# Sixteen-head attentions of a fused decoder: queries and keys projected without padded rows, each bank evicted twice

## Time and profile before

| | us |
|---|---|
| median of 3 runs | 2649.92 |
| lowest, highest | 2646.74, 2656.01 |
| profiled execution, own time | 2645.75 |
| its span (first to last instruction) | 2643.8 |
| PE busy in the span | 2145.4 (81%) |
| DVE busy | 1463.9 (55%) |
| ACT busy | 933.9 (35%) |
| POOL busy | 766.7 (29%) |

### The profile page before, as it was taken

The page is one execution under the profiler, slowest core; times in us unless marked ns, Lnnn a source line. Parts: engine busy times, 40 slices in busy tenths (PEclk is TensorE's granted clock), DMA queues, the critical chain, the costliest instruction groups (busy, mean ns, idle before and its releaser), DMA issues. The chain is left out here.

```text
span 2643.8 us, 37351 instructions
## 1 busy us (share of the span) xinstructions
PE 2145.4 (81%) x14118; PEld 1491.5 (56%) x14143; DVE 1463.9 (55%) x2966; ACT 933.9 (35%) x1539; POOL 766.7 (29%) x549
## 2 busy tenths in 40 slices
PE   7978857896498686499668877797999999687898
PEld 5765544564497575499345663485343434235787
DVE  4784773446432567311562454133799999993533
ACT  3423322331011234133323321111676667452543
POOL 1121231213200210100321011203489798973000
PEclk9999978998699687699789988898999999998899
DMA  4217010000697110698200002275201111001000
GB/s 161 73 41 248 17 34 32 1 2 33 236 358 297 58 33 8 233 358 320 66 1 25 1 2 89 80 213 154 88 25 40 31 34 40 25 1 52 1 17 16
DMA packets 104577, 234.22 MB, mean 89 GB/s; under 512 B 10000, under 2 KB 77456, under 8 KB 95440
## 3 DMA queue, kind: packets, MB, share of 16 engines
q1 hardware_dynamic: 95664, 209.81, 22.8%
q0 software_dynamic: 7680, 20.98, 2.4%
q10 hardware_dynamic: 1056, 1.05, 0.1%
HBM read 175.83 MB, written 55.97 MB: 88 GB/s over the span
## 5 line engine op out<-in xcount | busy, mean ns | idle before, releaser
L3631 POOL TENSOR_TENSOR l_attn_ring<-l_attn_ring,l_attn_c_rows 128x1024 f32<-128x1024 f32 x128 | 302.0, 2359 | 85.6 <-DVE l_attn_ring L3520 85.6
L3520 DVE TENSOR_TENSOR_SCAN l_attn_ring<-bank,l_attn_ring 128x512 f32<-128x512 f32 x256 | 299.2, 1210 | 22.6 <-ACT bank L3403 18.1
L164 PE MATMUL bank<-x_features,weights 128*128 128x512 f32 x544 | 260.5, 624 | 27.5 <-ACT x_features L3367 11.2
L3247 PE MATMUL bank<-l_attn_ring,identity 128*128 128x512 f32 x512 | 252.8, 617 | 36.8 <-POOL l_attn_ring L3631 29.8
L3403 ACT ACTIVATE bank<-l_attn_step,l_attn_minus_exp_a_log 128x508 f32<-128x508 f32 x256 | 173.5, 685 | 162.0 <-DVE l_attn_ring L3520 161.6
L164 PEld LDWEIGHTS bank<-x_features,weights 128*128 128x128 f32 x544 | 106.0, 199 | 155.5 <-issue 129.7
L3247 PEld LDWEIGHTS bank<-l_attn_ring,identity 128*128 128x128 f32 x512 | 96.6, 196 | 152.7 <-issue 105.2
L458 DVE TENSOR_REDUCE negmax_slots<-bank 128x16 f32<-128x2048 f32 x48 | 109.8, 2287 | 104.5 <-PE bank L350 104.2
L3514 DVE TENSOR_TENSOR l_attn_ring<-l_attn_step_times_input,bank 128x1024 f32<-128x1024 f32 x128 | 153.4, 1199 | 3.6 <-PE bank L3233 1.8
L3899 PE MATMUL bank<-l_ffn_hidden_high,l_ffn_sign_weights 128*128 128x512 f32 x256 | 99.7, 390 | 0.5 <-ACT l_ffn_hidden_high L3960 0.5
L3899 PE MATMUL bank<-l_ffn_hidden_low,l_ffn_sign_weights 128*128 128x512 f32 x256 | 99.6, 389 | 0.0
(11 more groups left out here) (678 smaller groups left out, 4486.4 us busy)
## 6 DMA issues: line engine op xcount, KB each, us to landing
l_attn_tile_weights<-l_ffn_experts SPq DMA_DIRECT2D x22, 2180.0 KB, 10.1
ffn_experts_tile_weights<-l_ffn_experts_experts SPq DMA_DIRECT2D x37, 1024.0 KB, 8.2
expert_slots<-zeros SPq DMA_DIRECT2D x8, 2048.0 KB, 13.6
l_attn_c_rows<-state_outputs SPq DMA_DIRECT2D x64, 256.0 KB, 3.2
l_ffn_tile_weights<-l_ffn_experts SPq DMA_DIRECT2D x23, 512.0 KB, 4.3
expert_slots<-residual_sum SPq DMA_DIRECT2D x62, 128.0 KB, 8.5
expert_slots<-zeros SPq DMA_DIRECT2D x1, 5888.0 KB, 27.8
l_ffn_tile_x<-expert_slots SPq DMA_DIRECT2D x23, 256.0 KB, 4.1
```

Source lines behind the costliest of these rows:

```text
L164: mm = pe.matmul(out, w[:, f, m * P:(m + 1) * P], src[:, f, :], start=start and f == 0, stop=stop and f == k - 1)
L3247: mm = pe.matmul(net.banks[SUMS[j]][:], net.ident[:], ring[n % 4][:, j, :], start=s == 0, stop=s == STATES - 1)
L3520: nc.vector.tensor_tensor_scan(ring[n % 4][:, j, :], net.banks[DECAY[j]][:], ring[n % 4][:, j, :], 0.0, ALU.mult, ALU.add).then_inc(state_ ...
L3631: tt(ring[n % 4][:], ring[n % 4][:], c_row[:, n % STATES, :].unsqueeze(1).broadcast_to([P, 2, T]), ALU.mult).then_inc(out_ready, 1)
```

## The change

The weights of queries and keys lose their padding. A projection of a group is 2 tiles u = 0, 1 of 128 rows. A tile holds 8 heads, laid so that each strip of 32 rows holds two heads side by side: rows 0 to 15 one of the even slot tile (t = 2u), rows 16 to 31 one of the odd slot tile (t = 2u + 1). ACT reads the bank twice and writes both slot tiles, each time with a per-partition scale `own` (1 for the rows of that tile's heads, 0 for the other rows) and, where there was a bias, the bias column. In the odd tiles the features lie in rows 16 to 31 and the shift row is row 0 of the slot; the buffer for the negated maxima is 16 columns longer and its transposes start 16 columns later for odd tiles. The pieces are spread anew: 2 at b = 0, 1 at b = 1, 1 at b = 2, and the values at b = 3 as before; four of them ahead of step 0. The layout of the values, the scores and all else stays.

```diff
+    def shift_at(self, t):
+        return t * P + (t % 2) * SHIFT_ROW
+
+    def take_slots(self, to, src, func, u, own, bias=None):
+        for t in (2 * u, 2 * u + 1):
+            kw = {} if bias is None else {"bias": bias[:, t:t + 1]}
+            ins = self.net.nc.scalar.activation(to[:, t, :], src, func, scale=own[:, t:t + 1], **kw)
+        return ins
...
-                    self.wait_taken(pe, self.number["q", g, 3])
+                    self.wait_taken(pe, self.number["q", g, 1])
...
-                                      net.negmax[k % 2][:, 4 * t:4 * t + 4, :].rearrange("p h s -> p (h s)"),
+                                      net.negmax[k % 2][:, self.shift_at(t):self.shift_at(t) + P],
...
-    return first + [(kind, g + 1, i) for kind, i in ((("k", 0), ("k", 1), ("k", 2)), (("k", 3), ("q", 0), ("q", 1)),
-                                                     (("q", 2), ("q", 3)), (("v", 0), ("v", 1)))[b]]
-FIRST_PIECES = [(kind, 0, m) for kind in "kq" for m in range(4)]
+    return first + [(kind, g + 1, i) for kind, i in ((("k", 0), ("k", 1)), (("q", 0),), (("q", 1),),
+                                                     (("v", 0), ("v", 1)))[b]]
+FIRST_PIECES = [(kind, 0, u) for kind in "kq" for u in range(2)]
...
-                        return nc.scalar.activation(heads.kT[g % 2][:, i, :], src, ACT.Relu,
-                                                    bias=w["one_rows"][:, 0:1])
-                    return nc.scalar.activation(heads.qT[g % 2][:, i, :], src, ACT.Relu)
+                        return heads.take_slots(heads.kT[g % 2], src, ACT.Relu, i, w["own"], w["one_rows"])
+                    return heads.take_slots(heads.qT[g % 2], src, ACT.Relu, i, w["own"])
... (the other two stages in the same way, with ACT.Identity, w["bk"] and w["bq"])
-            net.negmax = [room(f"negmax_slots{i}", [P, NH, SLOT]) for i in range(2)]
+            net.negmax = [room(f"negmax_slots{i}", [P, NH * SLOT + SHIFT_ROW]) for i in range(2)]
...
+def side_by_side(a):
+    import numpy as np
+    heads = a.reshape(*a.shape[:-1], 2, 2, 4, DH)
+    return np.ascontiguousarray(np.swapaxes(heads, -3, -2)).reshape(*a.shape[:-1], D)
```

More of the change, by code:

```diff
@@ L1187, in take @@
                     if kind == "k":
-                        return nc.scalar.activation(heads.kT[g % 2][:, i, :], src, ACT.Identity,
-                                                    bias=w["bk"][:, i:i + 1])
+                        return heads.take_slots(heads.kT[g % 2], src, ACT.Identity, i, w["own"], w["bk"])
                     if kind == "q":
-                        return nc.scalar.activation(heads.qT[g % 2][:, i, :], src, ACT.Identity,
-                                                    bias=w["bq"][:, i:i + 1])
+                        return heads.take_slots(heads.qT[g % 2], src, ACT.Identity, i, w["own"], w["bq"])
                     if kind == "c":
@@ L4277, in slots, with own_rows @@
     import numpy as np
-    out = np.zeros((*a.shape[:-1], NH, SLOT), a.dtype)
-    out[..., 0:DH] = a.reshape(*a.shape[:-1], NH, DH)
-    out[..., SHIFT_ROW] = row
+    out = np.zeros((*a.shape[:-1], 2, 2, 4, SLOT), a.dtype)
+    heads = a.reshape(*a.shape[:-1], 2, 2, 4, DH)
+    out[..., 0, :, 0:DH], out[..., 0, :, SHIFT_ROW] = heads[..., 0, :, :], row
+    out[..., 1, :, SHIFT_ROW:], out[..., 1, :, 0] = heads[..., 1, :, :], row
     return out.reshape(*a.shape[:-1], NH * SLOT)
+def side_by_side(a):
+    import numpy as np
+    heads = a.reshape(*a.shape[:-1], 2, 2, 4, DH)
+    return np.ascontiguousarray(np.swapaxes(heads, -3, -2)).reshape(*a.shape[:-1], D)
+def own_rows():
+    import numpy as np
+    return column(slots(np.ones(D, np.float32)))
 def parameters(i):
@@ L4299, in parameters @@
         "l0_xattn": [
-            ("wq", rows(slots(i["L0_xattn_Wq"].T))), ("wk", rows(slots(i["L0_xattn_Wk"].T))),
+            ("wq", rows(side_by_side(i["L0_xattn_Wq"].T))), ("wk", rows(side_by_side(i["L0_xattn_Wk"].T))),
             ("wv", rows(i["L0_xattn_Wv"].T)),
-            ("one_rows", column(slots(np.zeros(D, np.float32), 1.0)))],
+            ("one_rows", column(slots(np.zeros(D, np.float32), 1.0))), ("own", own_rows())],
     }
@@ L4306, in parameters @@
     out["l0_ffn_attention"] = [
-        ("wq", rows(slots(w0[:D].T))), ("wk", rows(slots(w0[D:2 * D].T))), ("wv", rows(w0[2 * D:].T)),
-        ("wo", rows(i0["out_proj_w"].T)), ("bq", column(slots(b0[:D]))), ("bk", column(slots(b0[D:2 * D], 1.0))),
+        ("wq", rows(side_by_side(w0[:D].T))), ("wk", rows(side_by_side(w0[D:2 * D].T))), ("wv", rows(w0[2 * D:].T)),
+        ("wo", rows(i0["out_proj_w"].T)), ("bq", column(slots(b0[:D]))), ("bk", column(slots(b0[D:2 * D], 1.0))), ("own", own_rows()),
         ("bv", spread(b0[2 * D:])), ("bo", spread(i0["out_proj_b"])),
@@ L4343, in parameters @@
     out["l2_xattn"] = [
-        ("wq", rows(slots(i["L2_xattn_Wq"]))), ("wk", rows(slots(i["L2_xattn_Wk"]))),
+        ("wq", rows(side_by_side(i["L2_xattn_Wq"]))), ("wk", rows(side_by_side(i["L2_xattn_Wk"]))),
         ("wv", rows(i["L2_xattn_Wv"])), ("wo", rows(i["L2_xattn_Wo"])),
-        ("bq", column(slots(i["L2_xattn_bq"]))), ("bk", column(slots(i["L2_xattn_bk"], 1.0))),
+        ("bq", column(slots(i["L2_xattn_bq"]))), ("bk", column(slots(i["L2_xattn_bk"], 1.0))), ("own", own_rows()),
         ("bv", spread(i["L2_xattn_bv"])), ("bo", spread(i["L2_xattn_bo"]))]
```

3 lines of the change are left out of this document (2 added, 1 removed).

## The result

| | median of runs | range | runs | ratio to before, 95% |
|---|---|---|---|---|
| before | 2652.97 us | 2646.74 to 2658.72 | 4 | |
| after | 2569.07 us | 2564.78 to 2576.28 | 4 | 0.969 [0.9667, 0.9713] |
| after again (e2) | 2575.96 us | 2571.80 to 2579.50 | 5 | 0.9712 [0.9689, 0.9735] |
| after once more (e11) | 2584.41 us | 2580.41 to 2584.88 | 5 | 0.974 [0.9725, 0.9755] |

What follows compares the result with a forecast made beforehand. PE's queue was taken as the bound; l2_xattn 23.8, l0_ffn_attention 24.4 and l0_xattn 20.8 us sum to 69, so 2649.9 becomes 2581 us. Its own range was 2573 to 2590, with part of the rivals 2570 to 2601.

Steps and rivals of the forecast that it cites:

- The start of the stages: Ahead of step 0 in each attention, four pieces go: 6.8 us, or 6.1 after the longer last pair.
- The bound and the unit price: PE's queue bounds the attentions; a query or key piece costs 1.71 us, and 48 removed pieces 82 us.
- The pair: ACT's two two-pointer evictions of one bank take 1.44 us together, 1.28 for the bias-free queries of l0_xattn.
- The tail: At a step's end the shifted scores wait for the last eviction pair: 0.31 us lost, 0.15 in l0_xattn.
- PE starts 0.05 later: In step 2 of l2_xattn, PE starts the shifted scores 0.05 us after its releaser ends, also behind a pair.
- The 0.28 us that I read for `l0_ffn_attention`: Before step 0 there, PE starts 0.28 us after its releaser; used for both the old and new start.
- DVE in l0_xattn: DVE's own shortest step is 7.28 us, 0.26 below the new 7.54 us step at b = 1; steps 6 and 10 win 0.
- The clock in steps 6 and 10: In l0_xattn PE's wait grows from 0.95 to about 2.7 us; the low clock costs 0.92 us in one step.
- Rival 1: The clock falls in 27 thinned attention steps, 0.92 us each, giving back 25 us: gain 44, 2606 us; 14%.
- POOL's chain: It moves with step 6 of l0_ffn_attention, costing nothing; the rival that it doesn't: gain 51, 2599 us, 4%.
- the remote wait: ACT's 8.71 us stall while POOL scatters rows may move, vanish or double: 8 us either way, 2573 to 2589; 7%.

Runs made afterwards that it cites:

- e2: The kernel after, unchanged, run again for a second profile: 2575.96 us, ratio 0.9712.
- e11: The kernel after, unchanged, once more on the same chip as e12: 2584.41 us, ratio 0.974.
- e1: The kernel before, unchanged, run again for a second profile: 2650.44 us.
- e3: Kernel after, with every query and key piece projected twice into its bank, evictions kept: 2653.53 us, ratio 1.0017.
- e8: Kernel after, with the second eviction pass left out from group 2 on, so odd heads keep older queries and keys: 2567.13 us, ratio 0.9713.
- e6: Kernel after, with ACT copying each bank to SBUF first and making both slot tiles from it, except a stage's first four pieces: 2572.39 us, ratio 0.9718.
- e4: Kernel after, with PE's last two waits exchanged, DVE's count first and ACT's last: 2577.60 us, ratio 0.9724.
- e5: Kernel after, with the pieces spread one, one and two instead of two, one and one: 2574.32 us, ratio 0.9729.
- e7: Kernel after, with the edits of e5 and e6 together: 2574.11 us, ratio 0.9722.
- e9: Kernel after, with unread filler transposes on PE ahead of long waits for the maxima in l0_xattn and l2_xattn: 2573.45 us, ratio 0.9704.
- e10: Kernel of e7 plus filler transposes in steps 12, 14, 15 of l0_xattn and step 15 of l2_xattn: 2568.42 us, ratio 0.9698.
- e12: The kernel of e10 once more, on the same chip as e11: 2567.38 us, ratio 0.9677.

## Why the prediction was right, step by step

The mechanism held: PE's queue was the bound, and the pieces taken out of it are the gain. That the sum came so near is in part luck, as the table shows: the steps fell short of the forecast, and the start and the ends of the stages gave more than I had counted. From the profiles before and after, us won:

| | forecast | measured |
|---|---|---|
| start and step 0, three stages | 7.5 each, 22.5 | 7.52 + 7.63 + 9.04 = 24.2 |
| steps 1 to 11, l0_xattn | 13.3 | 12.4 |
| steps 1 to 11, l0_ffn_attention | 16.9 | 16.1 |
| steps 1 to 11, l2_xattn | 16.3 | 14.8 |
| behind step 11, three stages | 0 | 0.3 + 2.0 + 2.5 = 4.8 |
| sum | 69 | 72.3 |

**The start of the stages: right, with luck.** The first profile before spent 29.00 us up to the shifted scores of step 0 of `l2_xattn`, e1 spent 27.66. The granted clock in their first 11.3 us was 0.73 and 0.85, and 0.87 in the profile after. So about 1.3 of the 9.04 us are the clock at the stage's head and not the change; the work that left is nearer to the 7.5 of the forecast.

**The bound and the unit price: right, shown.** A piece is worth 1.71 us of PE's queue; e3 puts it back and the time of before is back.

**The pair: right.** 1.45 us against 1.44. The Trainium skill ("ScalarE: Activation LUTs", section What ACT_TABLE_LOAD costs) would have made it an estimated 1.50; the row stands with the overlap of 0.10 that I read from the earlier trace rows.

**The tail: mis-sized.** I had 0.31 us a step (0.15 for queries of `l0_xattn`); it is 0.51 (e3, e8) and 0.33 (7.71 against 7.38 in e6). The step that failed is "PE starts 0.05 later": that was read from a release by DVE, the last in the list of waits. After ACT, with another wait behind it in the queue, PE came 0.26 later, and 0.15 with the order exchanged (e4). At the first scores, where no wait on DVE follows, it was 0.05 (1347.33 + 1.45, PE 1348.83). It costs about 0.2 us in each of 20 steps, 4 us, of which steps 6 and 10 of `l0_xattn` gave 0.7 back; all steps together fell 3.2 us short. The 0.28 us that I read for `l0_ffn_attention` in the earlier trace rows is a misreading: that row has 3 of its 4 matmuls, and at the same place after, with all 4, PE starts at 405.33, 0.05 us behind ACT's pair (403.83 + 1.45). It stood on both sides of my difference and changed nothing.

**DVE in l0_xattn: right.** b = 1 steps take 7.71 us, released by ACT, above DVE's own 7.28. Steps 6 and 10 are DVE's, and I had them winning nothing; they became 0.34 shorter, which agrees with the step ahead ending 0.33 later, beside DVE's chain.

**The clock in steps 6 and 10: right mechanism, counted as 0.92 once.** The clock fell in both; what it cost is in the steps behind them, 0.75 and 0.58. With a wait of 2.34 to 2.67 us ahead, 9 of 12 such steps lost the clock (after, e2, e4, e6, e8, e11); with more work, or filler, and a wait of at most 1.03 us none of 16 did (before, e1, e3, e5, e7, e9, e10, e12). e9 adds nothing to these steps but idle transposes on PE, so it is PE's own idleness.

**Rival 1, the clock in thinned steps:** it did not happen where PE waits 1.09 and 0.87 us, as in the thinned steps of the other two attentions (0.98 and 1.00). The Trainium skill ("TensorE: Matmul & The Clock Gate", section HAM oscillation) tells of a clock lost anew behind each wait between bursts; the trace agrees for the two long waits for DVE and not for the short ones.

**POOL's chain, the remote wait: right and harmless.** Step 7 of `l0_ffn_attention` won 0.5 us instead of 0. The 2.0 us behind its step 11 I have not traced; that stretch differs by 2.1 us among the three profiles of the kernel after (192.0, 193.6, 194.1), so they need not come from the change.

**What I had left out: the ends of the stages.** Behind step 11 of `l2_xattn` the same work took 55.9 to 60.1 us in the profiles without filler; where I looked into it, the difference went with the clock (0.77 and 0.78 over the last 25 us in after and e8, 0.68 and 0.64 in e5 and e6). Windows over its last steps and output pieces, before and after:

```profile
1559.00:1595.00 36.00, 19.79 (x212) 16.23 (x212) 17.27 (x58) 6.69 (x7) 4.84 (x4) 0.74 0.00 1
```

```profile
1485.00:1518.40 33.40, 17.38 (x212) 14.43 (x212) 17.17 (x58) 6.68 (x7) 4.84 (x4) 0.81 0.00 1
```

PE has the same count of matmuls, and 2.6 us went. The three executions of the kernel after agree (55.9 to 56.0), the two of the kernel before less so (58.5 and 60.1); e3 and e8 had 55.95, and e4 to e7 58.7 to 59.6. So it hangs on something that edits ahead of it shift, perhaps only the moment at which the stretch begins; that was not shown. It is one reason why e4 to e7 won step by step and not in the total, and a term of up to 4 us that my range should have held. With filler (e9, e10, e12) the stretch took 55.4, 55.2 and 55.3.

For the profiled execution the forecast was 2577, and 2564.78 was measured. Of these 12 us the three stages are 3.3 and the rest of the span 8.8: 1851.6 us, against 1859 to 1870 in all other profiles. What varies there I have not traced. No edit touched it, so this part is luck, and it put the first measurement below the range.

## What to carry to other kernels

Price a removed piece of work from two steps that differ in nothing else, and its last use from the wait that it hands over to, with that engine's own delay. When a step sheds work, look at PE's longest wait in it: moving work into that step, or even idle transposes, kept the clock here (`l0_xattn` 171.4 us, then 169.2 and 167.9). Small gains can be given back in a stretch behind them, so judge them by step and stage, and by a pair run on one chip.

## What the runs showed of the hardware that I had not expected

- PE starts 0.05 us after a release by the last wait in its queue, 0.26 after one with another, satisfied wait behind it, 0.15 with the two exchanged (e4).
- A pair of two-operand passes takes 1.45 us out of PSUM and 1.52 out of SBUF (e6).
- Twelve useless transposes (1.47 us) in a wait made the two steps that it touches shorter, 19.21 us instead of 19.96 (e9; in e2 steps 10 and 11 took 19.20 without it, as the clock held there).
- The low clock appeared behind waits of 2.34 to 2.67 us in the middle of a stage in 9 of 12 steps, and behind one of 1.65 us in 1 of 3 (e9, not e10 and e12).
